# Edge products two chunks at a time with a block-diagonal weight, and the small steps of the edge pass moved to VectorE

## The chip, the cores and the metric

The kernel runs on one core of a Trainium2 chip. The time is device microseconds of one launch, and lower is better. The engines are TensorE (PE: matrix products, with PEld for its weight loads), VectorE (DVE), ScalarE (ACT), GpSimd (POOL) and SyncE (SP), which here issues DMAs. They run side by side and wait for each other on semaphores.

## The reference

The program is a graph network on 3125 nodes with 256 features and 100000 edges sorted by their target. Each edge has 64 features and a weight. The two parts that matter here, shortened:

```python
# layer 0: weighted sum of the source rows of each target
msgs = edge_vals[:, None] * x[edge_src]
agg  = segment_sum(msgs, edge_dst)

# layer 1: edge attention, 8 heads of 32
ep     = edge_features @ We + be                    # [edges, 32], one row for all heads
scores = einsum('ehd,ehd->eh', q[dst], k[src] + ep[:, None, :]) * 32**-0.5 * ew[:, None]
m      = segment_max(scores, dst)
ex     = exp(scores - m[dst])
attn   = ex / segment_sum(ex, dst)[dst]
out    = segment_sum(attn[:, :, None] * v[src], dst) @ Wo + bo
```

Around them stand batch norms, two mixtures of experts, a linear attention over all nodes and two feed-forward networks; they are not touched, but for one of the feed-forward networks (the "mix layer": relu(x W1 + b1) W2 + b2, added to x), whose tiles are worked off inside the edge attention.

## The kernel before, in words

Nodes stand in 25 tiles of 128 rows. The edges are laid out in 416 chunks of 256 (an *item*), each of which belongs to one tile of target nodes; an item is two *subchunks* of 128 edges. Sixteen subchunks, so eight items, make a *window*, and there are 52 windows.

**Aggregation (`stage_aggregate`, 80 to 1395 us).** For each subchunk GpSimd gathers 128 source rows with an indirect DMA (L821) into a ring of 32 places, ScalarE multiplies them by the edge weight (L834), VectorE writes a 128x128 membership matrix that says which edge goes to which row of the tile (L876), TensorE multiplies the two into a sum (L993) and VectorE adds it to the accumulator (L885). GpSimd waits for the semaphore `summed` before it overwrites a place of the ring. Beside this TensorE multiplies the edge features by `We` (L983, in `edges`): 65 rows, 64 of features and one of ones for the bias `be`, times a weight of 65x32, one product per subchunk, in batches of eight. Batch b + 1 is issued ahead of the sums of batch b, in TensorE's one row of instructions. ScalarE copies a batch to SBUF (L842), SP writes it to memory and loads the next features (into one of two buffers, for two batches at a time, 64 rows of 4 KB). In several places the products of layer 0's linear attention are put between the items.

**The middle stage (`stage_mid`, 1395 to 2215 us)** computes q, k and v, with biases from `b_s`; k and v go to memory as one row of 512 numbers per node.

**Edge attention (`stage_flash`, 2215 to 4005 us).** A *body* treats two windows at once: the scores of window s and the softmax and sums of window a = s - 1. GpSimd gathers the k and v rows of the window after (L2821, 16 gathers), into one of two halves of a ring. For window s TensorE spreads q to the edges (`ask`, L2863), VectorE adds `ep` to the keys (L3074), multiplies (L3081), reduces to dots (L3085) and scales them to `scaled` (L3093). For window a, with one row per head and subchunk (8 x 16 = 128) and one column per edge:

- TensorE transposes `scaled` (L2891); VectorE scans for the running maximum of each segment (`within`) and writes `z`, the ends of each row.
- TensorE turns these to 8 rows of 16 subchunks (L2907, "ends"). VectorE scans over the subchunks (`across`: L3113 forward into `run`, L3115 backward into `back`), and gets `carry` and `fall`; the semaphore is `chain_ready`.
- TensorE spreads `carry` back over the 128 rows. It adds a `bar`, a large negative number wherever row and column don't match, so that a maximum over the row picks the right entry: L2913 with the identity puts the bar into PSUM and L2914 adds the product.
- VectorE takes that maximum (`lower`: L3125) and the larger of it and the row's own maximum (L3130): `p_ready`.
- TensorE computes the difference of `scaled` and the maximum, transposed back: L2929 (identity times `scaled`) and L2930 (`top` times minus the identity) into one PSUM tile, and L2931, the factor by which sums of the tile so far are rescaled, from `first_hot` and `diag`. ScalarE takes the exponential of all (L3017).
- VectorE rescales the accumulator and weighs the rows (L3138, L3143), TensorE sums them by membership (`collect` L2876, `fold` L2883) and ScalarE keeps the sums (L2992). The sums free the ring half that GpSimd waits for.

Small pieces are spread over the other engines: GpSimd writes `first_hot` (`hot`, L2830) ahead of each window's gathers, ScalarE writes `diag` and copies the last value of `run` to its front (L3014, L3015), so that the running maximum goes on in the next window.

In the same body half a tile of the mix layer's feed-forward network is worked off: `up` products, relu, then `down` (L2920 puts `work`, the row that the result is added to, into PSUM through the identity, four L2922 add half of the hidden features), and ScalarE copies PSUM back to `work` (L3030). Two bodies make a tile.

The order on each engine is that of the code: `body` is written out for each engine, and nothing is reordered. On TensorE it is: transpose of `scaled`; `up` products; the ends product (waits for `z_ready`); `ask(s, 0)`; bar and carry (wait for `chain_ready`); `down`; the products ahead of the exponential (wait for `hot_ready`, `diag_ready`, `p_ready`); `ask(s, 1)`; then `collect` and `fold`.

## Time and profile before

| | us |
|---|---|
| median of 3 runs | 4554.33 (4537.87 to 4564.51) |
| the profiled execution | 4516.46, its span 4514.7 |
| aggregation | 80 to 1395 |
| middle stage with mix layer | 1395 to 2215 |
| edge attention | 2215 to 4005 |
| last layers | 4005 to 4515 |
| busy: TensorE products, weight loads | 3317.5, 2604.1 |
| busy: VectorE, ScalarE, GpSimd | 2078.5, 1691.8, 1936.8 |

The busy time of the page counts a product from its issue to its modelled end. A group of the page ends with the idle time just ahead of its instructions on that engine, and with what ended it: "<-PE agg_sums L993" is a product of that line, "<-remote" a semaphore whose sender the profile doesn't name, "<-issue" time for which it shows no wait. In a timeline neighbouring instructions of one line are drawn together ("x16"), and the bracket is the idle time ahead of them. A TensorE instruction in this float32 kernel often stands as several records: "x2" for one product of L2913 is such a case. The granted clock of TensorE is written as a share of 2.4 GHz.

### The profile page before, as it was taken

To read this page: it belongs to the slowest core of one execution; us is meant where nothing else is said; L and a number is where in the kernel's file an instruction comes from. 1 tells how busy PE (TensorE), PEld (TensorE's weight loads), DVE (VectorE), ACT (ScalarE), POOL (GpSimd) and SP (SyncE) were. 2 spreads that over 40 slices of the span, in tenths; PEclk is the share of its full clock that TensorE was granted. 3 is DMA by queue.
4 is the path that set the end of the run, shared out by engine and by line. 5 is a ranking of instruction groups with operands and counts; after the bars stand their busy time and mean duration, and the time that the engine had idled before them with its cause. 6 is when DMAs were issued, how large, how long until landed. Compare 5 with 4: busy or idle time off the path is not lost. (4 is left out here: it accounts for less than half of the span.)

```text
span 4514.7 us, 52765 instructions
## 1 busy us (share of the span) xinstructions
PE 3317.5 (73%) x13864; PEld 2604.1 (58%) x13864; DVE 2078.5 (46%) x4472; ACT 1691.8 (37%) x4079; POOL 1936.8 (43%) x1903
## 2 busy tenths in 40 slices
PE   2666666676768599597477777787777777778978
PEld 2455555555555587464366666566666566556656
DVE  5232333232234500555456665565656555564424
ACT  1233232222233122333345544454544444444323
POOL 3565665565662044010544544444445444442010
PEclk8777766676768599897688888888888888889989
DMA  5443444444441166510655555555555555531000
GB/s 143 111 117 106 122 129 111 115 118 111 119 122 35 58 212 212 168 66 21 179 145 145 157 154 150 158 147 143 153 148 163 144 156 147 143 115 54 1 22 29
DMA packets 345537, 547.33 MB, mean 121 GB/s; under 512 B 170928, under 2 KB 222389, under 8 KB 344967
## 3 DMA queue, kind: packets, MB, share of 16 engines
q0 software_dynamic: 113216, 348.74, 27.6%
q1 hardware_dynamic: 224312, 183.42, 14.0%
q10 hardware_dynamic: 7743, 12.07, 0.8%
q8 instruction: 114, 1.87, 0.2%
q14 instruction: 152, 1.25, 0.1%
HBM read 493.32 MB, written 51.90 MB: 121 GB/s over the span
## 5 line engine op out<-in xcount | busy, mean ns | idle before, releaser
L2821 POOL DMA_INDIRECT store<-kv_d,src_of x832 | 880.1, 1058 | 937.6 <-PE flash_sums L2883 686.6
L821 POOL DMA_INDIRECT agg_rows<-xn_d,src_of x832 | 792.1, 952 | 524.7 <-issue 243.6
L993 PE MATMUL agg_sums<-agg_rows,agg_member 128*128 128x257 f32 x1664 | 524.9, 478 | 112.0 <-issue 78.4
L885 DVE TENSOR_TENSOR acc<-acc,agg_sums 128x257 f32 x416 | 176.5, 424 | 824.6 <-remote 556.4
L993 PEld LDWEIGHTS agg_sums<-agg_rows,agg_member 128*128 128x128 f32 x1664 | 394.3, 245 | 202.9 <-issue 92.1
L983 PE MATMUL agg_edge<-agg_we,agg_feats 65*128 65x32 f32 x1664 | 266.7, 306 | 263.2 <-issue 246.8
L2876 PE MATMUL flash_sums<-store,flash_member 128*128 128x264 f32 x1664 | 427.1, 390 | 14.8 <-issue 14.8
L983 PEld LDWEIGHTS agg_edge<-agg_we,agg_feats 65*128 65x128 f32 x1664 | 275.3, 241 | 275.7 <-issue 261.6
L2863 PE MATMUL flash_query<-q,flash_mem_t 128*128 x1664 | 413.2, 392 | 17.2 <-issue 16.4
L2876 PEld LDWEIGHTS flash_sums<-store,flash_member 128*128 128x128 f32 x1664 | 313.5, 191 | 84.7 <-issue 33.3
L842 ACT ACTIVATE agg_ep<-agg_edge 128x256 f32<-128x256 f32 x104 | 39.1, 376 | 847.4 <-remote 738.1
L834 ACT ACTIVATE agg_rows<-agg_rows,weight_of 128x256 f32<-128x256 f32 x832 | 342.8, 498 | 26.6 <-DMA agg_rows<-xn_d,src_of 23.5
L2863 PEld LDWEIGHTS flash_query<-q,flash_mem_t 128*128 128x128 f32 x1664 | 313.5, 194 | 66.7 <-issue 19.3
L2913 PE MATMUL flash_small<-flash_bar,ident 128*128 128x32 f32 x104 | 30.7, 387 | 381.5 <-DVEq L3121 333.0
L2883 PE MATMUL flash_sums<-acc,ident 128*128 x832 | 271.9, 409 | 22.5 <-issue 20.9
L3081 DVE TENSOR_TENSOR store<-store,flash_query 128x1024 f32<-128x1024 f32 x208 | 252.5, 1214 | 33.8 <-PE flash_query L2863 19.9
L3074 DVE TENSOR_TENSOR store<-store,flash_ep 128x1024 f32<-128x1024 f32 x208 | 253.5, 1219 | 23.1 <-issue 10.7
L2983 ACT ACTIVATE flash_member<-lane,lane_of 128x128 f32<-128x128 f32 x832 | 264.0, 395 | 0.0
L3143 DVE TENSOR_TENSOR store<-store,flash_pa 128x1056 f32<-128x1056 f32 x208 | 259.2, 1268 | 0.0
L2992 ACT ACTIVATE acc<-flash_sums 128x264 f32 x416 | 159.6, 384 | 257.4 <-PE flash_sums L2883 198.7
L2913 PEld LDWEIGHTS flash_small<-flash_bar,ident 128*128 128x128 f32 x104 | 25.3, 296 | 399.8 <-DVEq L3121 347.6
L3085 DVE TENSOR_REDUCE flash_dots<-store 128x32 f32<-128x1024 f32 x208 | 247.8, 1212 | 1.8
(480 smaller groups left out, 5222.9 us busy)
## 6 DMA issues: line engine op xcount, KB each, us to landing
moe_w<-in_L_ffn_W_dram SPq DMA_DIRECT2D x64, 512.0 KB
agg_feats<-in_ef_t_dram SPq DMA_DIRECT2D x104, 256.0 KB
flash_goal<-goal_d SPq DMA_DIRECT2D x52, 512.0 KB
agg_rows<-xn_d,src_of POOLq DMA_INDIRECT x832
ep_d<-agg_ep SPq DMA_DIRECT2D x52, 256.0 KB
store<-kv_d,src_of POOLq DMA_INDIRECT x832
flash_ep<-ep_d SPq DMA_DIRECT2D x416, 32.0 KB
flash_flags<-flags_d SPq DMA_DIRECT2D x416, 32.0 KB
```

Source lines behind the costliest of these rows:

```text
L821: pool.indirect_dma_start(rows[:, q, 0:D], None, sh.xn_d, bass.IndirectOffsetOnAxis(ap=sh.src_of[:, c:c + 1], axis=0)).then_inc(gathered[u ...
L834: act.activation(rows[:, q, 0:D], rows[:, q, 0:D], ACT.Copy, scale=sh.weight_of[:, bass.ds((UI * i + u) * SUBS + k, 1)]).then_inc(weighted, 1)
L983: last = pe.matmul(edge[:, p, c * DH:(c + 1) * DH], feats[:, p, c * P:(c + 1) * P], we_s[:, :], start=True, stop=True)
L993: last = pe.matmul(sums[:, j % 4, 0:W], member[:, c % (2 * BI * SUBS), :], rows[:, c % NB, :], start=(c % SUBS == 0), stop=(c % SUBS == SU ...
L2821: pool.indirect_dma_start(ring[:, s, :], None, sh.kv_d, bass.IndirectOffsetOnAxis(ap=sh.src_of[:, c:c + 1], axis=0)).then_inc(gathered[p][ ...
L2863: last = pe.matmul(query[:, c * D:(c + 1) * D], mem_t[:, g % 2, c * P:(c + 1) * P], sh.q[:, bass.ds(t, 1), :], start=True, stop=True)
L2876: pe.matmul(sums[:, n % 3, 0:W], member[:, g % 2, c, :], ring[:, a.side * WS + 4 * g + c, HI_], start=(k == 0), stop=False)
L2883: pe.matmul(sums[:, n % 3, 0:W], sh.ident[:, :], sh.acc[:, bass.ds(tiles[n], 1), :, :].rearrange("p a h v -> p (a h v)"), start=False, sto ...
L2983: act.activation(member[:, g % 2, k, :], sh.lane[:, :], ACT.Abs, scale=-1.0, bias=sh.lane_of[:, bass.ds(WS * a.at + (4 * g + k), 1)])
L3074: dve.tensor_tensor(r, r, ep[:, s.side, 4 * g:4 * g + 4, :].unsqueeze(2).to_broadcast([P, 4, H, DH]), ALU.add).then_inc(add_done, 1)
L3081: dve.tensor_tensor(r, r, query[:, :].rearrange("p (k f) -> p k f", k=4), ALU.mult).then_inc(mult_done, 1)
L3143: dve.tensor_tensor(r, r, e.unsqueeze(3).to_broadcast([P, 4, H, VW]), ALU.mult).then_inc(pv_ready, 1)
```

## The change

In the aggregation the weight `we_s` becomes a 128x64 block-diagonal matrix: `We` in the upper left and again in the lower right, zero elsewhere. The features of two subchunks stand above each other in 128 rows, so each `edges` batch is four products of 64 columns in place of eight of 32. A features load is two DMAs of 64 rows x 2 KB. ScalarE's copy puts the subchunks back in order, so that what goes to memory has the same layout. The bias no longer goes through the row of ones: it is added once to the bias of the keys in the middle stage.

In the edge attention the three products with a constant matrix leave TensorE. The bar is added by VectorE (`picked`); the difference is taken by VectorE (`low`) and one transpose takes it back; `work` no longer goes through PSUM, but `down` gathers both halves of a tile and VectorE adds it once, at the end of every second body. `first_hot`, `diag` and the copy of `run` are VectorE's, and the semaphores `hot_ready` and `diag_ready` go. `z` is written in two instructions, the first ahead of the drain of the backward scan.

```diff
...
-                sp.dma_start(we_s[0:ED, :], we).then_inc(loaded, 16)
-                sp.dma_start(we_s[ED:ED + 1, :], be).then_inc(loaded, 16)
+                sp.wait_ge(cleared, 1)
+                for h in range(2):
+                    sp.dma_start(we_s[h * ED:(h + 1) * ED, h * DH:(h + 1) * DH], we).then_inc(loaded, 16)
                 unsorted = sp.value_load(sh.unsorted[0:1, 0:1], min_val=0, max_val=P)
 
                 def feats_load(n, p):
-                    with sp.If(unsorted == 0):
-                        sp.dma_start(feats[0:ED, p, :], ef_t[:, bass.ds(n * WE, WE)]).then_inc(feats_in[p], 16)
-                    with sp.If(unsorted != 0):
-                        sp.dma_start(feats[0:ED, p, :], sh.ef_p[:, bass.ds(n * WE, WE)]).then_inc(feats_in[p], 16)
+                    for of, met in ((ef_t, unsorted == 0), (sh.ef_p, unsorted != 0)):
+                        with sp.If(met):
+                            for h in range(2):
+                                sp.dma_start(feats[h * ED:(h + 1) * ED, p, :], of[:, bass.ds(n * WE + h * (WE // 2), WE // 2)]
+                                             ).then_inc(feats_in[p], 16)
...
-                                act.activation(ep[:, n, p * HE:(p + 1) * HE], edge[:, p, 0:HE], ACT.Copy
-                                               ).then_inc(ep_ready, 1)
+                                act.activation(ep[:, n, p * HE:(p + 1) * HE].rearrange("p (h c d) -> p h c d", h=2, d=DH),
+                                               edge[:, p, 0:HE].rearrange("p (c h d) -> p h c d", h=2, d=DH), ACT.Copy).then_inc(ep_ready, 1)
...
-                dve.memset(feats[ED:ED + 1, :, :], 1.0).then_inc(loaded, 1)
+                dve.memset(we_s[:, :], 0.0).then_inc(cleared, 1)
...
-                    pe.wait_ge(feats_in[p], 16 * (b // 2) + 16)
+                    pe.wait_ge(feats_in[p], 32 * (b // 2) + 32)
                     if b >= 2:
                         pe.wait_ge(ep_ready, b - 1)
-                    for c in range(WS // 2):
-                        last = pe.matmul(edge[:, p, c * DH:(c + 1) * DH], feats[:, p, c * P:(c + 1) * P],
+                    for c in range(WS // 4):
+                        last = pe.matmul(edge[:, p, 2 * c * DH:2 * (c + 1) * DH], feats[:, p, c * P:(c + 1) * P],
...
+                key_b = b_s[:, D:2 * D].rearrange("p (h d) -> p h d", h=H)
+                dve.tensor_tensor(key_b, key_b, be_s[:, :].unsqueeze(1).to_broadcast([P, H, DH]), ALU.add)
+                dve.drain()
...
-                def hot(a):
-                    p = a % 2
-                    pool.wait_ge(flags_in[p], 16 * (H + 1) * (a // 2 + 1))
-                    if a >= 2:
-                        pool.wait_ge(back_ready, a - 1)
-                    pool.tensor_scalar(first_hot[:, p, :], sh.lane[0:H, :], steps[:, p, 4 * WS:4 * WS + 1], None, ALU.is_equal
-                                       ).then_inc(hot_ready, 1)
-
-                for w in range(NW):
-                    if w >= 1:
-                        hot(w - 1)
-                    gather(w, w % 2)
-                hot(NW - 1)
+                for i in range(0, NW // 2):
+                    for p in range(2):
+                        gather(2 * i + p, p)
...
-                        pe.matmul(carried, sh.ident[:, :], bar[:, :, :].rearrange("p a j -> p (a j)"), start=True, stop=False)
                         pe.matmul(carried, head_row[:, :], carry[:, :, :].rearrange("h a j -> h (a j)"),
-                                  start=False, stop=True).then_inc(carry_ready, 1)
+                                  start=True, stop=True).then_inc(carry_ready, 1)
                     if ffn is not None:
                         pe.wait_ge(hidden_ready, 2 * i + (half + 2))
-                        if 2 * i + half > 0:
-                            pe.wait_ge(down_added, 2 * i + half)
-                        pe.matmul(down[:, 0:D], sh.ident[:, :], sh.work[:, i, :], start=True, stop=False)
+                        pe.wait_ge(down_added, i + 1)
                         for m in range(FB):
                             last = pe.matmul(down[:, 0:D], hidden[:, m, :], w2_s[:, half * FB + m, :],
-                                             start=False, stop=(m == FB - 1))
+                                             start=(half == 0 and m == 0), stop=(half == 1 and m == FB - 1))
                         last.then_inc(down_ready, 1)
                     if a is not None:
-                        pe.wait_ge(hot_ready, a.at + 1)
-                        pe.wait_ge(diag_ready, a.at + 1)
                         pe.wait_ge(p_ready, a.at + 1)
-                        pe.matmul(pt[:, 0:P], sh.ident[:, :], scaled[:, :], start=True, stop=False)
-                        pe.matmul(pt[:, 0:P], top, minus[:, :], start=False, stop=True)
-                        pe.matmul(pt[:, P:P + H], first_hot[:, a.side, :], diag[:, :], start=True, stop=True).then_inc(back_ready, 1)
+                        pe.transpose(pt[:, 0:P], low[:, :], sh.ident[:, :])
+                        pe.matmul(pt[:, P:P + H], first_hot[:, :], diag[:, :], start=True, stop=True).then_inc(back_ready, 1)
...
-                        act.wait_ge(chain_ready, a.at + 1)
-                        act.activation(diag[:, :], sh.ident[0:H, 0:H], ACT.Copy, scale=fall[:, 0:1]).then_inc(diag_ready, 1)
-                        act.activation(run[:, 0:1], run[:, WS:WS + 1], ACT.Copy)
...
-                    if ffn is not None:
-                        act.wait_ge(down_ready, 2 * i + (half + 2))
-                        act.activation(sh.work[:, i, :], down[:, 0:D], ACT.Copy).then_inc(down_added, 1)
...
-                    dve.drain()
-                    dve.tensor_tensor(z[:, :, :], own[:, :].unsqueeze(1).to_broadcast([P, 2, WS]),
-                                      outer.unsqueeze(2).to_broadcast([P, 2, WS]), ALU.mult).then_inc(z_ready, 1)
+                    dve.tensor_scalar(z[:, 0, :], own[:, :], ahead[:, P - 1:P], None, ALU.mult)
+                    dve.drain()
+                    dve.tensor_scalar(z[:, 1, :], own[:, :], top[:, 0:1], None, ALU.mult).then_inc(z_ready, 1)
 
                 def across(a):
 
...
                                            ALU.add, ALU.max)
                     dve.tensor_tensor_scan(back[:, WS - 1::-1], steps[:, a.side, 4 * WS - 1:3 * WS - 1:-1],
                                            ends[:, 2 * WS - 1:WS - 1:-1], -BIG, ALU.add, ALU.max)
+                    dve.tensor_scalar(first_hot[:, :], sh.lane[0:H, :], steps[:, a.side, 4 * WS:4 * WS + 1], None, ALU.is_equal)
                     dve.drain()
                     dve.tensor_tensor(carry[:, 0, :], steps[:, a.side, 0:WS], run[:, 0:WS], ALU.add)
                     dve.tensor_tensor(carry[:, 1, :], steps[:, a.side, 2 * WS:3 * WS], back[:, 1:WS + 1], ALU.add)
                     dve.tensor_scalar(fall[:, :], run[:, 0:1], back[:, 0:1], 0.0, ALU.subtract, ALU.min)
                     dve.drain().then_inc(chain_ready, 1)
+                    dve.tensor_scalar(diag[:, :], sh.ident[0:H, 0:H], fall[:, 0:1], None, ALU.mult)
+                    dve.tensor_copy(run[:, 0:1], run[:, WS:WS + 1])
 
                 def lower(a):
                     dve.wait_ge(carry_ready, a.at + 1)
-                    dve.tensor_reduce(sides[:, :], carried.rearrange("p (a j) -> p a j", a=2), AX.X, ALU.max)
+                    dve.tensor_tensor(picked[:, :, :], carried.rearrange("p (a j) -> p a j", a=2),
+                                      bar[:, :].unsqueeze(1).to_broadcast([P, 2, WS]), ALU.add)
+                    dve.drain()
+                    dve.tensor_reduce(sides[:, :], picked[:, :, :], AX.X, ALU.max)
                     dve.drain()
                     for n in range(2):
-                        if n == 1:
-                            dve.drain()
-                        last = dve.scalar_tensor_tensor(out=top, in0=flags[:, a.side, 2 + n, :], scalar=sides[:, n:n + 1],
-                                                        in1=top, op0=ALU.add, op1=ALU.max)
-                    last.then_inc(p_ready, 1)
+                        dve.scalar_tensor_tensor(out=top[:, :], in0=flags[:, a.side, 2 + n, :], scalar=sides[:, n:n + 1],
+                                                 in1=top[:, :], op0=ALU.add, op1=ALU.max)
+                        dve.drain()
+                    dve.tensor_tensor(low[:, :], st, top[:, :], ALU.subtract).then_inc(p_ready, 1)
...
+                    if ffn is not None and ffn[1] == 1:
+                        i = ffn[0]
+                        dve.wait_ge(down_ready, 2 * i + 3)
+                        w = sh.work[:, bass.ds(i, 1), :].rearrange("p a f -> p (a f)")
+                        dve.tensor_tensor(w, w, down[:, 0:D], ALU.add).then_inc(down_added, 1)
...
```

On TensorE, one body of the edge attention, from the ends product to the last product ahead of the exponential, stood before the change (`flash_carry` and `flash_bar` are the carry and the bar above, `flash_down` the PSUM tile of the mix layer's feed-forward network):

```order
L2907 MATMUL flash_small<-flash_z,flash_row_head 8x32
L2863 ISA
L2863 MATMUL flash_query<-q,flash_mem_t 128x256 x2
L2863 ISA
L2863 MATMUL flash_query<-q,flash_mem_t 128x256 x2
L2913 MATMUL flash_small<-flash_bar,ident 128x32
L2914 MATMUL flash_small<-flash_carry,flash_head_row 128x32
L2920 MATMUL flash_down<-work,ident 128x256
L2922 MATMUL flash_down<-flash_w,flash_hidden 128x256 x4
L2929 MATMUL flash_small<-flash_scaled,ident 128x128
L2930 MATMUL flash_small<-flash_minus,flash_ahead_top 128x128
L2931 MATMUL flash_small<-flash_diag,flash_first_hot 128x8
```

The same place now (lines are those of the changed kernel):

```order
L2902 MATMUL flash_small<-flash_z,flash_row_head 8x32
L2858 ISA
L2858 MATMUL flash_query<-q,flash_mem_t 128x256 x2
L2858 ISA
L2858 MATMUL flash_query<-q,flash_mem_t 128x256 x2
L2908 MATMUL flash_small<-flash_carry,flash_head_row 128x32
L2914 MATMUL flash_down<-flash_w,flash_hidden 128x256 x4
L2919 MATMUL flash_small<-ident,flash_low 128x128
L2920 MATMUL flash_small<-flash_diag,flash_first_hot 128x8
```

Three products are gone, L2913, L2920 and one of L2929 and L2930; nothing changes places.

On VectorE, from the scans over the subchunks to the first multiplication of the next window, stood:

```order
L3113 SCALAR_TENSOR_TENSOR flash_run<-flash_steps,flash_run,flash_small 8x16
L3115 SCALAR_TENSOR_TENSOR flash_back<-flash_steps,flash_small 8x16
L3118 TENSOR_TENSOR flash_carry<-flash_steps,flash_run 8x16
L3119 TENSOR_TENSOR flash_carry<-flash_steps,flash_back 8x16
L3120 TENSOR_SCALAR flash_fall<-flash_run,flash_back 8x1
L3074 TENSOR_TENSOR store<-store,flash_ep 128x4x256
L3125 TENSOR_REDUCE flash_sides<-flash_small 128x2
L3130 SCALAR_TENSOR_TENSOR flash_ahead_top<-flash_flags,flash_sides,flash_ahead_top 128x128 x2
L3081 TENSOR_TENSOR store<-store,flash_query 128x4x256
```

Behind the two scans stands now:

```order
L3097 TENSOR_SCALAR flash_first_hot<-lane,flash_steps 8x128
L3099 TENSOR_TENSOR flash_carry<-flash_steps,flash_run 8x16
L3100 TENSOR_TENSOR flash_carry<-flash_steps,flash_back 8x16
L3101 TENSOR_SCALAR flash_fall<-flash_run,flash_back 8x1
L3103 TENSOR_SCALAR flash_diag<-ident,flash_fall 8x8
L3104 COPY flash_run<-flash_run 8x1
L3056 TENSOR_TENSOR store<-store,flash_ep 128x4x256
L3108 TENSOR_TENSOR flash_picked<-flash_small,flash_bar 128x32
L3111 TENSOR_REDUCE flash_sides<-flash_picked 128x2
L3114 SCALAR_TENSOR_TENSOR flash_top<-flash_flags,flash_sides,flash_top 128x128 x2
L3117 TENSOR_TENSOR flash_low<-flash_small,flash_top 128x128
L3063 TENSOR_TENSOR store<-store,flash_query 128x4x256
```

`first_hot` comes ahead of the carry, `diag` and the copy of `run` behind it, `picked` and `low` around the maximum; the addition to `work` (L3168) stands at the end of every second body, behind the scaling of the dots.

## Rows read from the trace of the kernel before

**Rows 1.** The page: span and number of instructions.
```profile
span 4514.7 us, 52765 instructions
```

**Rows 2.** Busy us by stage (PE, PEld, DVE, ACT, POOL), granted clock, DMA share, GB/s.
```profile
...
80.00:1395.00 1315.00, 871.81 (x3593) 719.89 (x3593) 389.08 (x1314) 382.08 (x971) 792.13 (x832) 0.71 0.44 117
...
2215.00:4005.00 1790.00, 1367.67 (x5937) 1102.32 (x5936) 1089.95 (x1450) 883.04 (x2202) 866.41 (x842) 0.86 0.53 149
```

**Rows 3.** Costliest groups in the aggregation stage, 80 to 1395 us.
```profile
...
L821 POOL DMA_INDIRECT agg_rows<-xn_d,src_of x832 | 792.1, 952 | 524.7 <-issue 243.6 <-remote 180.5 <-PE agg_sums L993 84.5
...
L983 PE MATMUL agg_edge<-agg_we,agg_feats 65*128 65x32 f32 x1664 | 266.7, 306 | 263.2 <-issue 246.8 <-DMA agg_feats<-in_ef_t_dram 15.6 <-DVE agg_mix_z L933 0.6
```

**Rows 4.** Timeline of GpSimd there: start, duration, line, instruction, idle before.
```profile
...
688.14 0.94 POOL L821 DMA_INDIRECT agg_rows<-xn_d,src_of  x1 [2.70 <-remote]
...
707.06 0.94 POOL L821 DMA_INDIRECT agg_rows<-xn_d,src_of  x1 [0.30 <-issue]
711.65 0.94 POOL L821 DMA_INDIRECT agg_rows<-xn_d,src_of  x1 [3.65 <-remote]
```

**Rows 5.** Timeline of TensorE there.
```profile
...
674.86 3.46 PE L983 MATMUL agg_edge<-agg_we,agg_feats 65*128 65x32 f32 x16
...
699.59 0.19 PE L983 MATMUL agg_edge<-agg_we,agg_feats 65*128 65x32 f32 x1 [0.65 <-issue]
...
717.59 1.87 PE L983 MATMUL agg_edge<-agg_we,agg_feats 65*128 65x32 f32 x16
```

**Rows 6.** Longest waits in the flash stage: us in total, times, longest.
```profile
...
POOL store L2821 <- PE flash_sums L2883: 686.6, 55, 16.9
DVE flash_run L3113 <- remote: 432.3, 43, 11.2
...
ACT flash_pa L3017 <- PE flash_small L2931: 274.2, 50, 7.4
```

**Rows 7.** Timeline of one flash window, four engines.
```profile
...
2995.43 0.22 PE L2907 MATMUL flash_small<-flash_z,flash_row_head 128*8 128x32 f32 x2
...
3003.07 0.96 POOL L2821 DMA_INDIRECT store<-kv_d,src_of  x1 [0.30 <-issue]
...
3005.99 0.24 DVE L3113 TENSOR_TENSOR_SCAN flash_run<-flash_steps,flash_run,flash_small 8x16 f32<-8x16 f32 x1 [10.62 <-remote]
...
3006.83 0.64 PE L2913 MATMUL flash_small<-flash_bar,ident 128*128 128x32 f32 x2 [9.21 <-DVEq L3121]
...
3007.40 0.63 PE L2914 MATMUL flash_small<-flash_carry,flash_head_row 8*128 8x32 f32 x2
...
3007.96 1.22 PE L2920 MATMUL flash_down<-work,ident 128*128 128x256 f32 x2
...
3008.33 0.78 DVE L3130 SCALAR_TENSOR_TENSOR flash_ahead_top<-flash_flags,flash_sides,flash_ahead_top 128x128 f32<-128x128 f32 x2
...
3008.97 3.62 PE L2922 MATMUL flash_down<-flash_w,flash_hidden 128*128 128x256 f32 x8
...
3012.39 0.64 PE L2929 MATMUL flash_small<-flash_scaled,ident 128*128 128x128 f32 x2
...
3013.33 0.38 PE L2931 MATMUL flash_small<-flash_diag,flash_first_hot 8*128 8x8 f32 x2
...
3013.75 0.28 ACT L3017 ACTIVATE flash_pa<-flash_small 128x136 f32<-128x136 f32 x1 [6.54 <-PE flash_small L2931]
```

**Rows 8.** Timeline of GpSimd after that window.
```profile
...
3019.71 1.56 POOL L2821 DMA_INDIRECT store<-kv_d,src_of  x1 [15.05 <-PE flash_sums L2883]
```

**Rows 9.** Timeline of TensorE in a window that found the clock up.
```profile
...
3257.89 1.89 PE L2922 MATMUL flash_down<-flash_w,flash_hidden 128*128 128x256 f32 x8
```

**Rows 10.** A small VectorE operation in the flash stage: xcount, busy us, mean ns.
```profile
...
L3125 DVE TENSOR_REDUCE flash_sides<-flash_small 128x2 f32<-128x32 f32 x50 | 9.6, 192 | 11.8 <-PE flash_small L2914 6.2 <-remote 5.1 <-issue 0.5
```

**Rows 11.** Timeline: a VectorE addition and a gather that start together.
```profile
...
2988.09 1.21 DVE L3074 TENSOR_TENSOR store<-store,flash_ep 128x1024 f32<-128x1024 f32 x1
2988.13 2.00 POOL L2821 DMA_INDIRECT store<-kv_d,src_of  x1 [0.30 <-issue]
```

44 lines of the change are left out of this document (21 added, 23 removed).

## The prediction

> **What bounds the kernel now.** I read the busy time by stage first [rows 1, 2]. Two stages carry the change: the aggregation (1315 us) and the flash stage with the edge attention (1790 us). In neither is an engine busy throughout: TensorE holds 66% and 76% of them, and its granted clock averages 0.71 and 0.86, so it is often at 1.2 GHz instead of 2.4. The question is then which wait closes each loop.
>
> In the aggregation I read the groups and then two timelines. GpSimd issues 832 gathers of 952 ns each with 525 us of idle time beside them, 792 + 525 = 1317 us, the whole stage [rows 3]. Its timeline shows bursts of 16 gathers at 1.25 us, then a pause: a burst begins at 688.14, its last gather at 707.06, the next burst at 711.65 [rows 4]. That is 23.5 us for 16 gathers, 18.9 of it issue and 4.6 from the last gather to the next burst. 36 bursts have exactly this form. Near the end of a burst TensorE's edge products stop flowing: 16 records take 1.87 us in a good place and 3.46 at the low clock, but from 699.59 on they come one by one with idle times of 0.5 to 2.6 us that the trace puts on nothing, until GpSimd has stopped [rows 5]. I can't say what causes it. What matters is that it ends with the burst, not with TensorE's work.
>
> In the flash stage I read the waits, then one window. GpSimd waits 687 us for the sums of TensorE, VectorE 432 us in 43 waits of about 10 us before L3113, ScalarE 274 us for the exp's input [rows 6]. The window shows the loop [rows 7, 8]: the product L2907 issues at 2995.43, but VectorE gets it at 3005.99 only, 2.9 us after GpSimd's last gather started (3003.07). I call 3005.99 R. TensorE has been idle for 9 us and its clock is down. From R on all is serial: VectorE's scans, TensorE's L2913, L2914, L2920, eight L2922, L2929 to L2931, then the exp at 3013.75 = R + 7.76. The next burst starts at 3019.71, 5.96 after the exp. In every window that I compared this distance is 5.9 to 6.0 us and that from the exp to the next `scaled` 16.3 us, whatever stands ahead. So time taken out between R and the exp comes out of the window whole, if the end of the next burst sets the next R.
>
> **The change part by part.** *Flash, TensorE.* Four products leave the path R to exp. L2913 costs 3007.40 - 3006.83 = 0.57 us; L2920 costs 3008.97 - 3007.96 = 1.01, of which some is the pipeline's start, which moves to the first L2922: I take 0.7. L2929 and L2930 cost 3013.33 - 3012.39 = 0.94 in four records; one transpose of one record replaces them, a quarter to a half of that, say 0.35: 0.6 saved. Sum 1.87 us at the low clock [rows 7]. At the high clock eight L2922 take 1.89 instead of 3.62 us [rows 9], so there the saving is about half, 0.9.
>
> *Flash, VectorE.* It gets `first_hot`, `diag`, the copy of `run`, `picked`, `low`, a split `z` and, in every other window, the addition to `work`. A small operation lasts 0.19 us and issues in about 0.1 [rows 10]; two of 128x128 (L3130) last 0.78, so one 0.39 [rows 7]. Ahead of `chain_ready` stands only `first_hot`, 0.15. Ahead of `p_ready` stand `diag` and the copy 0.2, `picked` with its drain 0.3, `low` with a drain 0.45: 1.1 us together, from 3009.11 (end of L3130) = R + 3.12 to R + 4.2. TensorE reaches this wait at R + 6.40 now (3012.39) and, 1.27 us earlier by L2913 and L2920 and 0.15 later by `first_hot`, at about R + 5.2 then. So `p_ready` is covered with 1 us to spare: no cost. If the drains cost twice what I take it is still covered; beyond that each 0.1 us costs 5 us in all.
> What `first_hot` delays (0.15) I subtract: 1.87 - 0.15 = 1.7 us a window.
> *Flash, in windows that find the clock up* the cover is gone: `p_ready` becomes the last, +1.1 - 0.9 = about +0.2 us, in 7 windows. Nothing.
> *The addition to `work`* (PSUM and SBUF, 128x256; nearest row 0.39 for 128x128; bounds 0.3 and 0.8) stands between `scaled` and the next window's scans, ahead of L2907. The burst is running there and ends 7 us later, so I take 0; if it counts, 25 x 0.45 = 11 us.
> *GpSimd and ScalarE* lose `first_hot`, `diag`, the copy of `run` and the copy of `down`. GpSimd's operation ran in its 15 us wait [rows 8], ScalarE's in waits as well: 0.
> Sum for flash: 43 windows x 1.7 = 73 us; in a few of them the clock comes back before the exp and less is saved: 70.
>
> The row on the gather beside a VectorE addition shows what more VectorE work could cost: a gather that starts at 2988.13, 0.04 us after L3074, takes 2.00 us instead of 0.95 [rows 7, 11]. The Trainium skill, "SBUF — State Buffer", "Who interferes with whom", says that VectorE and GpSimd share one pair of ports as an exclusive lock. By it every new VectorE operation could lengthen a gather; but the new ones stand between R and the exp, where GpSimd waits, and the sum stays.
>
> *Aggregation, TensorE.* 832 edge products of 32 columns become 416 of 64; the records halve from 1664 to 832. The trace has no 64-column product here. The bounds: the same price per record (the 32-column records go by the weight load, 1.87 / 16 = 0.117 us), or twice it. I take the same, since even records of 256 columns need only 1.89 / 8 = 0.24 us [rows 9]. A batch of 16 records then costs 0.94 us less at the high clock and 1.7 to 1.8 at the low one; over 104 batches TensorE issues 100 to 190 us less. Most of this meets no need. In a steady cycle GpSimd's burst of 16 takes 18.9 us however early TensorE is done, and the pause after it is the same; TensorE gives back slots early enough already. What remains are the stretches in which the ring is full and GpSimd waits for TensorE itself, as after the mix products: they end at 775.3 and then 3.62 us of edge products go first [rows 5]. There are 7 long pauses of this kind and some 10 shorter ones behind them: 7 x 1.8 + 10 x 0.9 = 22 us. I take 20. Bounds: 0, and all pauses gone, 36 x 3.4 + 22 = 145 us.
> *Aggregation, the rest.* The features come as two DMAs of 64 rows x 2 KB instead of one of 64 x 4 KB, the same bytes, loaded a batch or more ahead: 0. The ScalarE copy reads PSUM in another order, same count: 0. The bias moves into the middle stage, one VectorE addition and a small DMA: under 1 us.
>
> **Sum.** 70 + 20 = 90, less 2 for what is added: 88 us. The profiled execution took 4516.5 us (span 4514.7); it becomes 4428. The runs shown have a median of 4554.3; 4554.3 - 88 = **4466 us**, 1.9% less.
>
> **The rivals.** (1) *The aggregation opens up.* If TensorE's shorter edge work lets one or two more items through before it stalls, bursts grow beyond 16 and the pauses become fewer. For: a quarter of the products in that loop go. Against: the products behind the edges wait for VectorE's additions, which stand still in the same stretch. With half to all of the 145 us: 4554 - 70 - 110 = 4374.
> (2) *The gain is given back.* The 10.5 us wait at L3113 lasts a fixed time from L2907, or grows as the chain ahead shrinks, and nothing of the window comes out. For: the wait is unexplained, and 43 of 50 windows have nearly the same one. Against: the distances behind the exp are rigid. Time: 4554 - 20 = 4534, or up to 4554.
> (3) *Slower: VectorE's chain becomes last.* Place: `lower`, ahead of `p_ready`. Price: each microsecond by which VectorE comes after TensorE costs 50 us over 50 windows. It decides from R + 5.2 on, and outweighs all gains from about R + 7.3, so if the additions cost 4 us and not 1.1. Together with the addition to `work` on the path (+11), 5 us of additions give 4554 + 55 = 4609. Against: small operations in a row issue 0.1 us apart.
> (4) *The change doesn't do what it says*: the 64-column product costs two of 32 columns. Then the aggregation's 20 us go: 4486, inside my range.
>
> **How the numbers follow.** My forecast 0.60 (with its own range 4430 to 4500, and rival 4 in it), rival 1 0.14, rival 2 0.17, rival 3 0.09. What this measurement can tell from no change is about 0.5%, 23 us. Faster by more: 0.60 + 0.14 + a little of rival 2 = 0.77. Within: 0.15. Slower: 0.08. The range for 8 in 10 reaches into rivals 1 and 2: 4380 to 4545.
>
> **What would show it.** After the change, R to the exp should be about 6.0 us (7.76 now), the exp to the first gather still 5.96, the windows about 35 us instead of 36.9, and VectorE's `low` should end before TensorE's last L2914 of the new kernel. The wait before the scan of `run` should stay near 10 us. In the aggregation bursts of 16 at 23.5 us should persist, the edge records be half as many at 0.117 us, and the stage lose about 20 us. I am wrong if windows stay at 36.9, if the exp waits for `low`, or if the bursts change.

## The result: faster, and by more than forecast

| | before | after |
|---|---|---|
| median of 4 runs, us | 4546.1 (4532.85 to 4564.51) | 4341.6 (4336.3 to 4351.2) |
| ratio | | 0.956, 95% interval 0.953 to 0.959 |
| the profiled execution, us | 4516.5 | 4351.2 |

The forecast was 4466, with a range of 4380 to 4545. The change gained 204 us and not 88, and the time lies below the range. The two traces account for 165 of the 204: the recorded execution of the kernel before, 4516.5 us, is shorter than all four runs behind its median. A second comparison (e5 below) gave 4504.1 and 4337.6, 167 us apart. What the other 40 us of the first one were is in no trace; both gains are far from 88.

The stages of the changed kernel, with the columns of [rows 2] (the edge attention now ends near 3870, so its row is shorter), and the two groups of the aggregation that answer to [rows 3]:

```profile
...
80.00:1395.00 1315.00, 706.03 (x2761) 560.87 (x2761) 389.19 (x1313) 382.91 (x971) 792.85 (x832) 0.71 0.42 117
2215.00:3870.00 1655.00, 1324.29 (x5676) 1063.98 (x5676) 1175.09 (x1803) 865.85 (x2082) 823.54 (x801) 0.90 0.58 163
```

```profile
...
L824 POOL DMA_INDIRECT agg_rows<-xn_d,src_of x832 | 792.8, 953 | 522.7 <-issue 237.6 <-remote 178.8 <-PE agg_sums L996 90.7
...
L986 PE MATMUL agg_edge<-agg_we,agg_feats 128*128 128x64 f32 x832 | 116.9, 288 | 31.0 <-DMA agg_feats<-in_ef_t_dram 25.4 <-issue 5.0 <-DVE agg_mix_z L936 0.6
```

TensorE does 166 us less in the aggregation (706 for 872), and GpSimd's idle time there is the same, 522.7 for 524.7. The first gather of that stage starts at 80.3 and the last at 1379.2; before it was 80.6 and 1380.3. So in this pair of traces the stage has lost 1 us (over all traces it is more, see the section on the prediction). Nearly all of the gain is in the edge attention: its last gather starts at 3848.6, before at 4012.8, and these 164 us are nearly the 165 by which the profiled executions differ.

The longest waits of the edge attention now (us in total, times, longest), which answer to [rows 6]:

```profile
...
POOL store L2826 <- PE flash_sums L2878: 556.4, 82, 32.4
ACT acc L2981 <- remote: 287.6, 66, 6.8
...
DVE flash_run L3093 <- remote: 56.3, 7, 11.2
```

The wait of 10 us ahead of the scan of `run`, 43 times before, stands there 7 times, 8 us long on average. In its place ScalarE waits 66 times for something remote ahead of L2981, which keeps the sums of a tile. One window shows how (start, duration, engine, line, instruction, idle time ahead; compare [rows 7] and [rows 8]):

```profile
...
2575.34 0.28 ACT L3003 ACTIVATE flash_pa<-flash_small 128x136 f32<-128x136 f32 x1 [2.07 <-issue]
...
2581.56 1.22 POOL L2826 DMA_INDIRECT store<-kv_d,src_of  x1 [6.47 <-PE flash_sums L2878]
...
2586.84 1.20 POOL L2826 DMA_INDIRECT store<-kv_d,src_of  x1 [0.30 <-issue]
...
2587.14 1.22 DVE L3056 TENSOR_TENSOR store<-store,flash_ep 128x1024 f32<-128x1024 f32 x1
...
2594.71 0.39 ACT L2981 ACTIVATE acc<-flash_sums 128x264 f32 x1 [3.94 <-remote]
...
2595.35 1.04 PE L2878 MATMUL flash_sums<-acc,ident 128*128 x2 [2.58 <-issue]
...
2599.66 1.02 POOL L2826 DMA_INDIRECT store<-kv_d,src_of  x1 [2.68 <-remote]
...
2600.42 0.22 PE L2902 MATMUL flash_small<-flash_z,flash_row_head 128*8 128x32 f32 x2 [0.83 <-DVE flash_z L3088]
...
2600.68 0.23 DVE L3093 TENSOR_TENSOR_SCAN flash_run<-flash_steps,flash_run,flash_small 8x16 f32<-8x16 f32 x1 [0.32 <-issue]
...
2602.88 1.99 PE L2914 MATMUL flash_down<-flash_w,flash_hidden 128*128 128x256 f32 x8
...
2604.50 0.29 DVE L3117 TENSOR_TENSOR flash_low<-flash_small,flash_top 128x128 f32<-128x128 f32 x1
...
2604.85 0.33 PE L2919 MATMUL flash_small<-ident,flash_low 128*128 128x128 f32 x1
...
2605.53 0.28 ACT L3003 ACTIVATE flash_pa<-flash_small 128x136 f32<-128x136 f32 x1 [1.81 <-PE flash_small L2920]
```

The exp is at 2575.34 and the first gather 6.2 us later. Near the 8th gather TensorE's signals become late, as before, but now this hits the sums: ScalarE gets one at 2594.71 after 3.9 us, and TensorE's last `fold` (the adding up that frees places of the ring), at 2595.35, comes 20 us behind the exp. In the window of [rows 7] it comes 16.2 us behind it:

```profile
...
2976.53 0.28 ACT L3017 ACTIVATE flash_pa<-flash_small 128x136 f32<-128x136 f32 x1 [6.23 <-PE flash_small L2931]
...
2992.72 0.71 PE L2883 MATMUL flash_sums<-acc,ident 128*128 x2
```

GpSimd needs that fold for the 13th gather and stops; the gather starts at 2599.66. In this pause the signals flow again. TensorE's ends product issues at 2600.42, later than before, but VectorE has it 0.26 us later and not 10.6. The exp follows at 2605.53: a window of 30.2 us. Over 49 windows the mean distance of exps is 32.6 us; before it was 36.0. I call it a signal that is late, but the trace shows only when a product issues and when the engine behind it starts, so a product that ended late would look the same.

### The profile page after: what moved, and what is told of

Read it like the earlier page. It is cut to its first block and busy times, and to the rows that moved or that the text cites. A ratio compares the mean times of both kernels' runs of the same rounds, so it can differ in the third digit from the quotient of the medians.

```text
span 4349.4 us, 50720 instructions
## 1 busy us (share of the span) xinstructions
PE 3088.6 (71%) x12672; PEld 2389.1 (55%) x12672; DVE 2143.6 (49%) x4808; ACT 1662.7 (38%) x3925; POOL 1878.2 (43%) x1851
## 3 DMA queue, kind: packets, MB, share of 16 engines
q0 software_dynamic: 113216, 348.74, 28.2%
## 5 line engine op out<-in xcount | busy, mean ns | idle before, releaser
L2826 POOL DMA_INDIRECT store<-kv_d,src_of x832 | 854.2, 1027 | 841.2 <-PE flash_sums L2878 556.4
L824 POOL DMA_INDIRECT agg_rows<-xn_d,src_of x832 | 792.8, 953 | 522.7 <-issue 237.6
L996 PE MATMUL agg_sums<-agg_rows,agg_member 128*128 128x257 f32 x1664 | 515.2, 473 | 479.4 <-DVE acc L888 426.3
L2858 PE MATMUL flash_query<-q,flash_mem_t 128*128 x1664 | 445.5, 415 | 55.0 <-DVE store L3063 27.8
L2878 PE MATMUL flash_sums<-acc,ident 128*128 x832 | 283.4, 424 | 192.0 <-issue 174.1
L2858 PEld LDWEIGHTS flash_query<-q,flash_mem_t 128*128 128x128 f32 x1664 | 334.7, 207 | 114.0 <-issue 60.9
L2981 ACT ACTIVATE acc<-flash_sums 128x264 f32 x416 | 159.4, 383 | 548.3 <-remote 287.6
L2878 PEld LDWEIGHTS flash_sums<-acc,ident 128*128 128x128 f32 x832 | 151.5, 198 | 264.0 <-issue 247.7
L3128 DVE TENSOR_TENSOR store<-store,flash_pa 128x1056 f32<-128x1056 f32 x208 | 255.9, 1252 | 0.0
L879 DVE TENSOR_SCALAR agg_member<-lane,lane_of 128x128 f32<-128x128 f32 x832 | 181.7, 310 | 10.1 <-issue 1.5
L2963 ACT ACTIVATE flash_mem_t<-flash_goal,minus_row 128x512 f32<-128x512 bf16 x208 | 148.1, 712 | 34.5 <-issue 16.9
L2975 ACT ACTIVATE flash_member<-flash_member,ones 128x512 f32<-128x512 f32 x208 | 150.2, 722 | 14.9 <-issue 0.7
```

The costliest lines, as they stand in the source:

```text
L824: pool.indirect_dma_start(rows[:, q, 0:D], None, sh.xn_d, bass.IndirectOffsetOnAxis(ap=sh.src_of[:, c:c + 1], axis=0)).then_inc(gathered[u ...
L996: last = pe.matmul(sums[:, j % 4, 0:W], member[:, c % (2 * BI * SUBS), :], rows[:, c % NB, :], start=(c % SUBS == 0), stop=(c % SUBS == SU ...
L2826: pool.indirect_dma_start(ring[:, s, :], None, sh.kv_d, bass.IndirectOffsetOnAxis(ap=sh.src_of[:, c:c + 1], axis=0)).then_inc(gathered[p][ ...
L2858: last = pe.matmul(query[:, c * D:(c + 1) * D], mem_t[:, g % 2, c * P:(c + 1) * P], sh.q[:, bass.ds(t, 1), :], start=True, stop=True)
L2878: pe.matmul(sums[:, n % 3, 0:W], sh.ident[:, :], sh.acc[:, bass.ds(tiles[n], 1), :, :].rearrange("p a h v -> p (a h v)"), start=False, sto ...
L3128: dve.tensor_tensor(r, r, e.unsqueeze(3).to_broadcast([P, 4, H, VW]), ALU.mult).then_inc(pv_ready, 1)
```

## The experiments

The runs fell on several chips and times, and each is compared with the kernel before as measured beside it. Beside e1 to e4 that kernel took 3680 us, beside e5 to e14 4502 to 4508. I call the late signals the stall. In the traces of e1 to e4 it is not there at all: the scan of `run` starts at most 0.32 us behind its product. The same chip showed it later (e12 to e14), so it isn't the chip; what switches it on was not found. Each number below is told as one with the stall or without it.

**e1 and e2: one half of the change alone.** Both were measured without the stall. Their edits are the two halves of the diff above.

> Only the part of the change in the aggregation and the middle stage, on the kernel before. Theory (the stage is paced by GpSimd's bursts of 16 gathers and the pause behind them, whatever TensorE's edge products cost): first to last gather 1299 us as in both traces, the time within 5 us of before, about 4545. The forecast's step (the full-ring stretches shrink): 20 us less. Rival (the edge part opens something outside its stage, as the loads of the middle stage): 100 us or more of the gain come with it.

> Only the part of the change in the edge attention. Theory: nearly the whole gain, 4345 to 4355, windows of 32.6 us on average where they were 36.0, most of them with GpSimd's burst broken into 12 and 4 gathers and no wait of 10 us ahead of the scan of run. Rival (the gain needs both parts): 4460 to 4500.

Measured: 3682.1 and 3679.1, ratios 1.0004 (0.9995 to 1.0014) and 0.9999 (0.9989 to 1.0009). Neither could show what it was made for: the theories of both speak of a kernel with the stall, and without it the aggregation runs from first to last gather in 1047 us (e1) and 1044 (e2), and not in 1299. Their use is another: without the stall the change is worth nothing in the edge attention. 900 us of that stage, first in e1, which has it as before, then in e2, which has it as changed:

```profile
...
2200.00:3100.00 900.00, 887.33 (x4305) 727.81 (x4304) 790.21 (x1049) 638.32 (x1594) 674.16 (x615) 1.00 0.76 217
```

```profile
...
2200.00:3100.00 900.00, 858.34 (x4086) 691.92 (x4084) 836.62 (x1290) 621.77 (x1492) 611.62 (x584) 1.00 0.76 219
```

TensorE goes from 887 to 858 us busy and VectorE from 790 to 837; the windows take 24.9 and 24.7 us. That the gain is nothing because VectorE takes on what TensorE gives up fits these numbers, but no run without the stall tests it: e6 and e7 were to do so and met the stall. The aggregation of e1 also shows what the stall costs there:

```profile
...
L824 POOL DMA_INDIRECT agg_rows<-xn_d,src_of x832 | 795.0, 955 | 269.0 <-issue 241.2 <-POOLq L388 15.7 <-PE agg_sums L996 12.2
```

832 gathers in 1047 us with one pause, 269.0 us of idle time where [rows 3] has 524.7.

**e3 and e8: GpSimd held behind the 8th gather.** One wait in the kernel before:

```diff
                         hold(pool, sums_done, WI * w + (2 * g + 2), pool_ticks)
+                        if g == 2 and w > 0:
+                            pool.wait_ge(ends_ready, w)
```

> The kernel before with one more wait on GpSimd in the edge attention: behind the 8th gather of a window it waits for the ends product of the window at work (L2907), which TensorE issues 18.9 us after the exp; nothing else is changed. Theory (TensorE's signals get stuck from about the 9th gather of an unbroken burst on, until GpSimd pauses): the wait of 10.5 us ahead of the scan of run goes to under 1 us, although GpSimd is held 2 to 3 us longer and its last gather comes later; windows of 26 to 30 us, time 4200 to 4350. Rival (the wait comes from the amount of gather data ahead, or from the distance between exp and ends, and not from the burst): the scan still waits until about 3 us after the last gather, which now starts later: windows of 38 to 40 us, 4600 to 4700.

> The kernel before with GpSimd held behind the 8th gather of a window until the ends product of the window at work, once more, since the chip of its first run showed no stall to take away (there: 13 us slower). On a chip with the stall, theory (an unbroken burst of more than 8 gathers sets it off): windows of 26 to 30 us, 4200 to 4350. Rival: 4600 to 4700, as the last gather comes later. On a chip without it: 3693 again.

e3 had no stall to remove and came out 13 us slower, 3693.1 (1.0031, 1.0020 to 1.0043). e8, with the stall: 4093.6 us, ratio 0.911 (0.906 to 0.916). An added wait makes the kernel 410 us faster, a larger gain than I had expected (4200 to 4350 us), though the windows are in my range. GpSimd behind the 8th gather of a window of e8:

```profile
...
2563.49 1.22 POOL L2823 DMA_INDIRECT store<-kv_d,src_of  x1 [0.30 <-issue]
2565.95 0.95 POOL L2823 DMA_INDIRECT store<-kv_d,src_of  x1 [1.24 <-PE flash_small L2909]
2567.20 0.94 POOL L2823 DMA_INDIRECT store<-kv_d,src_of  x1 [0.30 <-issue]
```

The hold costs 1.24 us there, and the scan of `run` starts under 0.3 us behind its product in 44 of 52 windows and at most 1.05 us behind it in the others. The mean window is 27.6 us; 10 of 49 take under 25, as without the stall, and 24 take 28 or more, so short pauses don't clear it for good. The rival, by which the wait follows the last gather whatever its burst, is out: the last gather starts 31.3 us behind the exp and not 26.5 (medians), and the wait is gone.

**e5: the changed kernel again, and e6, e7: the change to the edge attention in two parts.** e6 is the changed kernel with `first_hot` back on GpSimd and `diag` and the copy of `run` back on ScalarE. e7 is the kernel before with only these three on VectorE, as in the diff above, and every product still on TensorE. Of e7 (e6 is its reverse, on the changed kernel):

```diff
-                    if w >= 1:
-                        hot(w - 1)
                     gather(w, w % 2)
...
+                    dve.tensor_scalar(first_hot[:, a.side, :], sh.lane[0:H, :], steps[:, a.side, 4 * WS:4 * WS + 1], None, ALU.is_equal)
                     dve.drain()
...
                     dve.drain().then_inc(chain_ready, 1)
+                    dve.tensor_scalar(diag[:, :], sh.ident[0:H, 0:H], fall[:, 0:1], None, ALU.mult)
+                    dve.tensor_copy(run[:, 0:1], run[:, WS:WS + 1])
```

> The changed kernel itself, once more, on whatever chip this lands. What is known: on the chip of the first comparison the ratio to before was 0.956, on the chip of the last experiments either half of the change moved nothing and the kernel before took 3680 us. Theory (the gain comes out of the stall of TensorE's signals late in a burst of gathers, which that second chip doesn't show): where before takes about 4550, a ratio of 0.956; where it takes about 3680, 1.000. Rival (the two halves together do what neither does alone): 0.96 on either chip.

> The changed kernel with first_hot on GpSimd and diag and the copy of run on ScalarE again, as before; the three products stay away from TensorE. On a chip without the stall, theory (VectorE's row of work is what closes the window of 24.8 us there, and takes back what TensorE saves): 0.25 to 0.35 us a window come back, 12 to 18 us, 3662 to 3668. Rival (TensorE closes the window): no difference, 3680. On a chip with the stall: theory (what matters is when the first gathers of a window start against VectorE's additions) about as the changed kernel, 4340 to 4400; rival (taking first_hot off GpSimd made the gain): 4450 or more.

> The kernel before with first_hot, diag and the copy of run on VectorE; all products stay on TensorE, and the aggregation is that of before. On a chip without the stall: theory (VectorE closes the window) 15 us slower, 3695; rival (TensorE closes it) 3680. On a chip with the stall: theory, as before with windows of 36 to 37 us, 4545; rival (first_hot off GpSimd made the gain) 4350 to 4400.

| with the stall | us | ratio to before (4504.1) |
|---|---|---|
| e5, all of the change | 4337.6 | 0.964 (0.959 to 0.969) |
| e6, products away, small steps where they were | 4340.6 | 0.965 (0.961 to 0.970) |
| e7, products all there, small steps on VectorE | 4337.2 | 0.964 (0.959 to 0.969) |

Either part alone gives the whole gain. e6 fell where its theory had it (4340 to 4400). My theory for e7, "as before", was wrong; its rival (`first_hot` off GpSimd made the gain, 4350 to 4400) came near, but e6, with `first_hot` on GpSimd, excludes it as the only cause. That sends the question back: what do a shorter row of products and three moved trifles have in common? A window of e7:

```profile
...
2554.92 0.28 ACT L2998 ACTIVATE flash_pa<-flash_small 128x136 f32<-128x136 f32 x1 [2.37 <-PE flash_small L2915]
...
2566.43 0.95 POOL L2818 DMA_INDIRECT store<-kv_d,src_of  x1 [0.30 <-issue]
2566.46 1.22 DVE L3055 TENSOR_TENSOR store<-store,flash_ep 128x1024 f32<-128x1024 f32 x1
...
2579.07 1.02 POOL L2818 DMA_INDIRECT store<-kv_d,src_of  x1 [2.55 <-remote]
...
2579.92 0.24 DVE L3094 TENSOR_TENSOR_SCAN flash_run<-flash_steps,flash_run,flash_small 8x16 f32<-8x16 f32 x1 [0.32 <-PE flash_small L2893]
...
2585.48 0.28 ACT L2998 ACTIVATE flash_pa<-flash_small 128x136 f32<-128x136 f32 x1 [2.35 <-PE flash_small L2915]
```

The 5th gather starts at 2566.43, VectorE's addition at 2566.46. The gather is ahead by 0.03 us and takes 0.95. In the kernel before it was behind by 0.04 us and took 2.00 [rows 11]. The kernel before has windows of the other kind too, such as this one:

```profile
...
3372.06 0.28 ACT L3017 ACTIVATE flash_pa<-flash_small 128x136 f32<-128x136 f32 x1 [6.59 <-PE flash_small L2931]
...
3383.63 1.27 DVE L3074 TENSOR_TENSOR store<-store,flash_ep 128x1024 f32<-128x1024 f32 x1
3383.64 0.94 POOL L2821 DMA_INDIRECT store<-kv_d,src_of  x1 [0.30 <-issue]
...
3396.21 1.02 POOL L2821 DMA_INDIRECT store<-kv_d,src_of  x1 [2.87 <-remote]
...
3397.06 0.23 DVE L3113 TENSOR_TENSOR_SCAN flash_run<-flash_steps,flash_run,flash_small 8x16 f32<-8x16 f32 x1 [0.32 <-PE flash_small L2907]
```

Here the gather is behind by 0.01 us only and takes 0.94. GpSimd then stops ahead of the 13th gather (2.87 us), and the scan waits 0.32 us. The two halves of the change do this in two ways. e7 starts the 5th gather earlier, 11.50 us behind the exp for 11.60, and the addition stays where it was. e6 leaves the gather and in about half of the windows starts the addition 0.1 us or more behind it.

So I sorted the windows of all kernels with the stall and without the hold in two ways, by the start of the 8th gather counted from the exp, and by the time from the 1st gather to the 8th. I asked whether the burst breaks (over 2.4 us from the 12th to the 13th gather). Each cell has the broken bursts of all, in 49 windows; worked out from the records:

| kernel | 8th later than 15.95 us | 8th earlier | 1st to 8th 10.4 us or more | 1st to 8th 9.7 us or less |
|---|---|---|---|---|
| before | 0 of 44 | 5 of 5 | 0 of 44 | 5 of 5 |
| after | 6 of 11 | 37 of 38 | 0 of 4 | 43 of 45 |
| e5 | 0 of 4 | 44 of 45 | 0 of 4 | 44 of 45 |
| e6 | 3 of 22 | 22 of 27 | 0 of 17 | 25 of 32 |
| e7 | 0 of 4 | 45 of 45 | 0 of 4 | 45 of 45 |
| e10 | 9 of 30 | 18 of 19 | 0 of 20 | 27 of 29 |
| e12 | 0 of 49 | | 0 of 49 | |
| e13 | 14 of 45 | 4 of 4 | 0 of 28 | 18 of 21 |

The second sort is the cleaner one: no burst breaks whose first eight gathers took 10.4 us or more, and 207 of the 222 others do. In between there is nothing: a single gather that takes 2.00 us in place of 0.95 puts a window on the other side. (The late 8th gathers that break all belong to bursts that began as a whole some 7 us or more behind the exp and not 6.) Both limits, 15.95 and the gap between 9.7 and 10.4, were set after the traces had been seen.

The form of the burst is not the whole gain, though. In e6 25 bursts break, with windows of 30.9 us, and 24 don't, with windows of 34.2, where the kernel before has 44 unbroken ones of 36.5. So about a third of e6's gain comes from unbroken windows that are shorter (24 x 2.3 = 55 us of 49 x 3.5 = 170), as fits a shorter row of products, while e7 has 45 broken windows of 31.8 and only 4 others.

**e10 and e12: the 5th gather pushed back.** The changed kernel with one (e10) or two (e12) idle operations on GpSimd:

```diff
                         hold(pool, sums_done, WI * w + (2 * g + 2), pool_ticks)
+                        if g == 1:
+                            if w > 0:
+                                pool.wait_ge(idled, w)
+                            pool.iota(idle_i[:, :], pattern=[[1, 256]], base=0, channel_multiplier=0).then_inc(idled, 1)
```

> The changed kernel with one small operation on GpSimd (an iota of 128x256, about 0.4 us) ahead of the 5th gather of each window. In the traces of the slow windows the 5th gather starts 11.6 us after the exp, just behind the start of VectorE's addition, takes 2.0 us, and the 8th starts at 16.4; in the fast windows the 5th starts at 11.5, ahead of that addition, takes 1.0 to 1.2 us, and the 8th starts at 15.3 to 15.5. Theory (this hair's breadth decides whether the stall begins before or behind the last fold, and so whether GpSimd is stopped after 12 gathers or goes on to 16): with the operation the 5th gather starts at about 12, takes 1.5 us or more, the 8th starts behind 16.3, bursts of 16 come back and with them windows of 36 us: 4480 to 4540 on a chip with the stall, 3680 to 3700 on one without. Rival (the shorter row of products or GpSimd's freedom of first_hot made the gain): 0.4 us x 50 = 20 us slower at most, 4360.

> As the last test of the 5th gather, with two of the small operations on GpSimd in place of one: one moved the 5th gather of a window from 11.51 to 11.75 us behind the exp only, still ahead of VectorE's addition at 11.80, and in the windows in which it did get behind it the bursts of 16 were back. Two of 0.36 us should put it at about 12.1, inside the addition. Theory (an 8th gather later than 16 us behind the exp means a burst of 16 and the wait): 8th gather at 16.4 or later in nearly all windows, at least 40 of 49 bursts unbroken behind the 12th gather, windows of 35 to 36.5 us: 4470 to 4530 on a chip with the stall, 3690 to 3710 on one without. Rival (the late 8th gather goes with the long window but doesn't make it): windows of 33 to 34 us, 4380 to 4400.

e10: 4363.8, ratio 0.967 (0.960 to 0.974). By its numbers the rival won, but the push was too short: the 5th gather moved from 11.51 to 11.75 us behind the exp, and only in part of the windows behind the addition. e12: 4411.4, ratio 0.978 (0.973 to 0.983). A window of it:

```profile
...
2552.87 0.28 ACT L3010 ACTIVATE flash_pa<-flash_small 128x136 f32<-128x136 f32 x1 [5.20 <-PE flash_small L2927]
...
2564.07 0.77 POOL L2829 IOTA flash_idle_i<- 128x256 int32 x2
...
2564.41 1.22 DVE L3063 TENSOR_TENSOR store<-store,flash_ep 128x1024 f32<-128x1024 f32 x1
...
2565.00 1.45 POOL L2833 DMA_INDIRECT store<-kv_d,src_of  x1 [0.16 <-issue]
...
2579.34 0.94 POOL L2833 DMA_INDIRECT store<-kv_d,src_of  x1 [0.30 <-issue]
...
2582.30 0.23 DVE L3100 TENSOR_TENSOR_SCAN flash_run<-flash_steps,flash_run,flash_small 8x16 f32<-8x16 f32 x1 [10.36 <-remote]
...
2588.11 0.28 ACT L3010 ACTIVATE flash_pa<-flash_small 128x136 f32<-128x136 f32 x1 [6.95 <-PE flash_small L2927]
```

```profile
...
DVE flash_run L3100 <- remote: 351.8, 42, 10.5
```

The 5th gather starts inside the addition and takes 1.45 us, no burst of the 49 breaks, and the wait is back, 42 times and 8.4 us long on average. So a first half of the burst that is 1 us longer makes the form of the burst and does not only go with it. Part of that 1 us is the two idle operations themselves, so e12 doesn't single out the meeting with the addition. The time lies between what theory (4470 to 4530) and rival (4380 to 4400) had: the windows take 34.4 us on average, not 35 to 36.5. The unbroken windows of the kernel before take 36.5, so here the change is worth 2.1 us a window: 1.5 of it from the scan of `run` to the exp (6.1 us for 7.7, medians), the rest in shorter waits.

**e9: the hold in the changed kernel**, first run as e4 without the stall.

> The changed kernel with the same extra wait on GpSimd behind the 8th gather. Theory: bursts of 8 and 8, last fold again 16.3 us after the exp in place of 21.5, ends product at about 19, windows of 25 to 29 us, time 4050 to 4250. Rival: GpSimd held longer only delays its last gather, windows of 34 us or more, 4400 or more.

> The changed kernel with GpSimd held behind the 8th gather of a window until that window's ends product, once more, since the chip of its first run showed no stall. On a chip with the stall, theory: the two gains add up only so far as the stall allows; the pause takes the stall away in both kernels, so about as the kernel before with the same pause, 4060 to 4100. Rival (change and pause are independent): 4094 - 170 = 3920. On a chip without the stall: 3684 again.

e4: 3683.7 (1.0009, 0.9999 to 1.0018), where theory had written 4050 to 4250 for a kernel with the stall. e9: 4130.4, ratio 0.917 (0.910 to 0.923). Change and hold act on the same thing and don't add: 3920 is out. The changed kernel is even a little behind e8; its windows take 28.8 us for 27.6, though the intervals of the two ratios overlap. It is also above the 4060 to 4100 that I expected. Why is open.

**e11: gathers further apart in the aggregation**, beside the hold.

```diff
+                            if c > 0:
+                                pool.wait_ge(idled, c)
+                            pool.iota(idle_i[:, :], pattern=[[1, 64]], base=0, channel_multiplier=0).then_inc(idled, 1)
                             pool.indirect_dma_start(rows[:, q, 0:D], None, sh.xn_d,
```

> The changed kernel with the pause behind the 8th gather, and in the aggregation a small operation on GpSimd (an iota of 128x64, about 0.2 us) ahead of each of the 832 gathers, so that they come every 1.45 us and not every 1.25. On a chip with the stall, theory A (gathers issued faster than something can take them up fill it, and the stall is its overflow): the pauses of 4.7 us behind every 16 gathers shrink or go, the stage takes 1210 to 1290 us in place of 1300, up to 90 us faster than without the operation. Theory B (an unbroken stretch of about 10 us of gathers sets it off, whatever their spacing): bursts stay, each 3 us longer, the stage takes 1350 us or more. On a chip without the stall: 832 x 0.2 = 166 us slower than e9 there, about 3850.

4119.9 us, ratio 0.914 (0.907 to 0.922). The operation of 0.2 us fitted for the most part into the 0.3 us between two gathers, which came every 1.31 us and not every 1.45. The pause shrank from 4.7 to 3.9 us, the cycle of 16 stayed at 23.7, and from first to last gather the stage took 1296 us for 1281 in e9. That decides neither theory: 1296 us is just above the range of A and far below that of B. At both spacings the stage gets 16 gathers in some 23.6 us.

**e13 and e14: SP's loads of edge products left out**, in the kernel before and in e8. From the third window on both take the edge products that lie in the buffer; only their time is used.

```diff
                     for n in range(WI):
+                        if not first:
+                            sp.sem_inc(ep_in[p], 16)
+                            continue
                         c = sp.value_load(sh.chunk_id[0:1, bass.ds(WI * w + n, 1)], min_val=0, max_val=NCH - 1)
```

> The kernel before; from the third window on the eight loads of edge products that SP issues for each window (8 x 32 KB in pieces of 256 bytes) are left out, so the scores use the wrong edge products; all waits stay. They start at about the 8th gather, where the stall begins, so they may be what sets it off. Theory A (SP's loads are the cause, or a good part of it): no stall, windows of 25 to 28 us, 3950 to 4100 on a chip with the stall. Theory B (the gathers alone are, as in the aggregation, which has no such loads): the wait ahead of the scan stays near 10 us, windows of 35 to 37 us, 4450 to 4510. On a chip without the stall: 3680.

> The kernel before with GpSimd held behind the 8th gather, and without the loads of edge products as in the last one. With the hold alone windows took 27.6 us on average, the good ones 24.7, the others 28 to 31. Theory A (the traffic of all queues fills what overflows): nearly all windows 24.7, 3920 to 3970 on a chip with the stall. Theory B (only the gathers do): 27.6 again, 4090. On a chip without the stall: 3690.

Measured 4349.3 (0.965, 0.960 to 0.970) and 3994.1 (0.886, 0.882 to 0.891). Two rows of e13, the first for the wait ahead of the scan:

```profile
...
DVE flash_run L3116 <- remote: 129.4, 26, 11.1
DVE flash_sides L3128 <- remote: 116.6, 27, 6.4
```

129 us in 26 waits, where [rows 6] has 432 in 43. But VectorE now also waits 117 us, 27 times, for something remote a few instructions on, ahead of the maximum over the row (L3128 there), where [rows 10] has 5.1. Both theories of e13 fall: the stall is shorter, windows of 32.8 us, but it is there. Broken and unbroken windows of e13 take the same time, 32.6 and 32.9 us. With the hold, e14 has windows of 25.7 us on average, 2 less than e8. Its 3994 us lie outside the ranges of both theories (3920 to 3970, and 4090), nearer to that of A. 1300 us of the edge attention, first e8, then e14:

```profile
...
2300.00:3600.00 1300.00, 1173.06 (x5577) 960.42 (x5575) 1027.66 (x1364) 827.71 (x2064) 862.35 (x800) 0.98 0.69 195
```

```profile
...
2300.00:3600.00 1300.00, 1229.17 (x5898) 1001.52 (x5898) 1087.69 (x1528) 884.97 (x2218) 907.91 (x811) 0.99 0.67 194
```

TensorE is busy 1173 and 1229 us, at granted clocks of 0.98 and 0.99. So the stall is there without SP's small pieces (256 bytes), and with them the kernels take some 100 to 150 us longer. How much of that is the stall is open, since no run without the stall leaves the loads out.

## Why the prediction was wrong

- *"In every window this distance is 5.9 to 6.0 us ... So time taken out between R and the exp comes out of the window whole, if the end of the next burst sets the next R."* This is the step that failed, at its condition. I took the unbroken burst of 16 as given. But 5 of 49 windows in the kernel before were of the other form, with a broken burst, no wait of 10 us and 31.4 us for 36.5; the change moved 43 of 49 into it. e12, which keeps all bursts unbroken, gives nearly half of the gain back (4411 us, for 4338 and 4502). I had written that the wait "should stay near 10 us" and that I was wrong "if the bursts change"; they did.
- *The 1.7 us a window.* Right for the form that I looked at: in unbroken windows the way from R to the exp takes 6.1 us for 7.7 (medians), and 6.0 in e6, which leaves the small steps where they were. e12, with all bursts unbroken, is 91 us faster than before (4411.4 for 4502.0), against a sum of 88. That the two agree so well is in part luck: e12 has two more operations on GpSimd, and its waits are shorter than before, which I had not forecast. In the broken form the products have little value: e7 saves none and is as fast as e5.
- *R to the exp.* Forecast 6.0 us. Over all windows the median is 5.6 in this trace and 6.2 in e5, the same kernel, for 7.6 before. In unbroken windows `low` ends 4.1 us behind R (forecast 4.2) and the last `down` product 5.4: covered, as written. In the broken ones TensorE's clock is up (eight records of L2914 take 1.99 us above), and the cover is nearly gone: `low` (to 2604.79 above) ends 0.1 us ahead of the last `down` product (2604.87), and in 19 of 43 such windows it ends behind it. I had written this for 7 windows at the high clock and not for 43. It costs little, TensorE waits 17 us in all for `low`, and rival 3 is out.
- *The exp to the first gather.* Forecast 5.96 as before, measured 6.23 in most windows. So this distance is less rigid than I had it.
- *The lock of VectorE on GpSimd.* I cited the rule (the Trainium skill, "SBUF — State Buffer", "Who interferes with whom") and the 2.00 us of [rows 11], and concluded that the sum stays, since the new operations stand where GpSimd waits. What I missed is that a shift of a few hundredths moves the old additions against the gathers. The page says that the instruction which starts first gets the ports and the other blocks. The traces agree roughly: a gather takes 0.95 us when 0.03 ahead of the addition and 2.00 when 0.04 behind it, but also 0.94 when 0.01 behind.
- *The aggregation, 20 us.* Measured 1 in the first pair of traces, where the seven long pauses behind the mix products sum to 95 us before and after (the first is 11.4 for 18.1 us, the sixth 15.8 for 9.2). One pair misleads here. From first to last gather the stage takes 1300 to 1311 us in the five traces with the stall and the old products (before, e7, e8, e13, e14) and 1281 to 1299 in the six with the new ones (after, e5, e6, e9, e10, e12), on average 1306 and 1289. That is 17 us, near the forecast; without the stall it is nothing (1044 to 1048 in e1 to e4). Between the long pauses the stage runs at 16 gathers in 23.6 us in any case. The edge records are half as many and take 116.9 / 832 = 0.14 us where they took 266.7 / 1664 = 0.16, so a product of 64 columns costs no more than one of 32. Rival 4 is out, and rival 1 as well: most of the pauses still stand behind bursts of 16.
- *The range.* Its lower end took the opening of the aggregation in and gave the edge attention nothing below its own sum, though its wait of 432 us was "unexplained" in my own words. An unexplained wait that some windows escape bounds the gain at its whole size. The 44 unbroken windows of before take 36.5 us on average and its 5 broken ones 31.4: 44 x 5.1 = 224 us.

## What to carry to other kernels

Where a wait has no cause that you can name, and some repetitions escape it, look first at what those have in common, and let the range reach as far as if all escaped. Sort the repetitions by the start of one instruction; a short table told more here than the sum of the durations. Read a stage's time from several traces where you have them: one pair said 1 us, eleven traces say 17. And be wary of a gain that either half of a change gives alone: a good part of it belongs to a threshold, which the next edit may cross back, so remove what stands behind it. With the stall, the one added wait of e8 (4094 us) is worth twice this change; without it, it costs 13 us.

## What the runs showed of the hardware

- With the stall, from about the 8th or 9th gather of an unbroken burst on, signals of TensorE reach other engines up to 11 us late [rows 6], and in the aggregation its instructions issue only now and then [rows 5]. It ends about 3 us after the last gather starts [rows 7]. Without it the same kernel runs in 3680 us. A gather takes 0.95 us either way (952 ns in [rows 3], 955 in e1).
- The stalled trace of the kernel before holds 30474 semaphore updates, that of e1 62642, for the same 113216 packets on GpSimd's queue; all stalled traces have under 31000 and the four others over 60000. The Trainium skill, "NOTIFIC — the notification-queue block", "Overflow: three behaviours, one of which stalls the engine", says that the block which writes event records can hold back the engines that produce them. That would fit records missing and signals late together, but no run here shows it, and it stays open. Every run here has a span and a granted clock, so each was recorded, and it is open too whether the stall is there in a launch without records.
- The Trainium skill, "SBUF — State Buffer", "Who interferes with whom", says that TensorE never waits on anyone. Of the ports that may be so; but in these traces what TensorE sends comes up to 11 us late while gathers run on, and e8, which interrupts them, takes that away.
